# A gated cross-attention layer on one core: the step of a software pipeline rewritten on all engines, its sums done by TensorE transposes

## The reference, cut to what matters

```python
# part 1, k = v = ctx, q = layernorm(x); i, j run over the 8 rows of a head
kv  = einsum('bhil,bhjl->bijhl', k, v)
y   = causal convolution of kv with ssm_kernel[h] along l (512 taps)
out = y + kv * D
out = einsum('bijhl,bhil->bjhl', out, q)
x   = x + tanh(g_xattn) * out
# part 2, over z = layernorm(x), 16 positions per batch row, 16 heads
y = silu(z_prev * w0 + z * w1)
q = silu(y @ Wq); k = y @ Wk; v = y @ Wv; g = y @ Wg
q, k = rotary(q), rotary(k)
scores = softmax(v . router_w); onehot = one_hot(argmax(scores))   # 2 routes
norm = 1 / cumsum(onehot)
q_exp = q * scores * onehot * norm ; k_exp = k * onehot
o = tril(q_exp k_exp^T / 4) v
o = (o - mean) / sqrt(var + 1e-5)
x = x + tanh(g_ffn) * ((silu(g) * o) @ Wout)
```

## Time and profile before

| | |
|---|---|
| median of three runs | 1350.26 us (1345.44 to 1352.43) |
| span of the profiled execution (the page gives no other time of it) | 1371.8 us |
| PE busy | 1227.0 us (89%) |
| DVE busy | 1080.5 us (79%) |
| POOL busy | 849.3 us (62%) |
| ACT busy | 391.8 us (29%) |
| mean granted TensorE clock | 0.826 of 2.4 GHz |

### The profile page before, as it was taken

The page is one execution under the profiler, slowest core; times in us unless marked ns, Lnnn a source line. Parts: engine busy times, 40 slices in busy tenths (PEclk is TensorE's granted clock), DMA queues, the critical chain, the costliest instruction groups (busy, mean ns, idle before and its releaser), DMA issues.

```text
span 1371.8 us, 18443 instructions
## 1 busy us (share of the span) xinstructions
PE 1227.0 (89%) x6272; PEld 992.6 (72%) x6272; DVE 1080.5 (79%) x1815; ACT 391.8 (29%) x809; POOL 849.3 (62%) x741
## 2 busy tenths in 40 slices
PE   2579999999999999999999999999999999999986
PEld 1456878776778767778767687777788777778774
DVE  5888787778787778977779876979877779877762
ACT  3432332222332213332213322322332222332220
POOL 5667675557675557765547754767765556765520
PEclk9887798887798868988868976988888888888887
DMA  6000111110011110111110011010011010010000
GB/s 202 24 24 1 31 32 31 32 31 1 30 31 31 31 31 0 31 31 31 31 31 1 29 31 31 31 31 18 12 31 31 31 31 23 7 32 23 9 8 16
DMA packets 21579, 39.00 MB, mean 28 GB/s; under 512 B 2288, under 2 KB 3440, under 8 KB 21552
## 3 DMA queue, kind: packets, MB, share of 16 engines
q1 hardware_dynamic: 17952, 33.92, 8.7%
q10 hardware_dynamic: 3600, 4.72, 1.1%
HBM read 30.17 MB, written 8.47 MB: 28 GB/s over the span
## 4 chain that ended last, share of the span: by engine, by line
DVE 35%; PE 29%; issue 19%; POOL 12%; ACT 4%; DMA 1%; DVEq 0%; POOLq 0%; SPq 0%; ACTq 0%
PE bank L287 9%; DVE z_terms L791 8%; PE bank L339 8%; PE bank L316 6%; PE bank L276 4%; PE bank L359 3%; DVE ke L805 3%; DVE z_terms L796 2%; DVE q_sel L930 2%; POOL kv L649 2%; POOL kv_low L658 2%; DVE weight L928 2%; DVE cnt L922 2%; POOL z_terms L673 2%; DVE z_terms L785 1%
## 5 line engine op out<-in xcount | busy, mean ns | idle before, releaser
L339 PEld LDWEIGHTS bank<-v_sb,att 128*128 128x128 f32 x1024 | 246.6, 300 | 20.3
L678 POOL TENSOR_TENSOR o_rstd<-o_ve,minus_half 128x16 f32<-128x16 f32 x32 | 93.0, 2907 | 224.5 <-DVE o_ve L831 224.5
L339 PE MATMUL bank<-v_sb,att 128*128 128x32 f32 x1024 | 206.1, 342 | 0.0
L658 POOL TENSOR_TENSOR kv_low<-kv,kv_high 128x576 fp32r<-128x576 f32 x128 | 203.0, 1587 | 0.0
L678 POOL TENSOR_TENSOR rstd<-ve,minus_half 128x1 f32<-128x1 f32 x64 | 35.0, 547 | 253.8 <-DVE ve L991 221.7
L649 POOL TENSOR_TENSOR kv<-kx 128x512 f32<-128x512 f32 x128 | 177.6, 1388 | 15.1 <-ACT kx L503 15.1
L791 DVE TENSOR_TENSOR z_terms<-z_terms 128x256 f32<-128x256 f32 (+1 forms) x160 | 180.1, 1141 | 4.5 <-POOL z_terms L673 0.7
L287 PE MATMUL bank<-kv_high,toep_high 128*128 128x512 f32 x320 | 170.2, 532 | 3.4 <-DVE z_terms L785 3.4
L534 ACT ACTIVATE o_sq<-bank 128x512 f32<-128x512 f32 x32 | 19.1, 598 | 504.0 <-PE bank L339 504.0
L287 PE MATMUL bank<-kv_low,toep_high 128*128 128x512 f32 x320 | 159.9, 500 | 0.0
L287 PE MATMUL bank<-kv_high,toep_low 128*128 128x512 f32 x320 | 158.1, 494 | 0.0
(11 more groups left out here) (112 smaller groups left out, 2520.0 us busy)
## 6 DMA issues: line engine op xcount, KB each, us to landing
c_in<-in_ctx SPq DMA_DIRECT2D x32, 256.0 KB
x_in<-in_x SPq DMA_DIRECT2D x32, 256.0 KB
toep<-taps_dram SPq DMA_DIRECT2D x32, 256.0 KB, 5.2
out_x<-out_sb SPq DMA_DIRECT2D x32, 256.0 KB
w_all<-in_L_ffn_Wv ACTq DMA_DIRECT2D x1, 1024.0 KB, 11.4
w_all<-in_L_ffn_Wg ACTq DMA_DIRECT2D x1, 1024.0 KB, 8.1
w_out<-in_L_ffn_Wout ACTq DMA_DIRECT2D x1, 1024.0 KB, 12.7
router<-in_L_ffn_router_w ACTq DMA_DIRECT2D x1, 512.0 KB, 7.0
```

The costliest lines, as they stand in the source:

```text
L339: ins = nc.tensor.matmul(bank[4][:, i * HDV:(i + 1) * HDV], att[:, r, c, :], v_sb[:, i * HDV:(i + 1) * HDV], start=True, stop=True)
L658: eng.tensor_tensor(kv_p[1][:, p, c, :], kv[:, c % 2, :], kv_p[0][:, p, c, :].bitcast(F32), ALU.subtract).then_inc(kv_ready[c], 1)
L678: eng.tensor_tensor(dst[:, 0:n], src[:, 0:n], minus_half[:, 0:n], ALU.pow).then_inc(done, 1)
```

## The change

The host lays out the context (reversed, transposed, extended), so that SP loads `kx` directly, in two buffers; the ACT reversal, the PE transposes and the ACT copies go. The taps are split in high and low once, before they go to DRAM, and one DMA per step (twice the bytes) brings both; L508 and L667 go. The sums of `z_terms` on DVE and POOL go: PE transposes all eight blocks of each chunk, 32 transposes, accumulating in PSUM. The attention output is formed transposed: stationary `v_sb` 128x32, moving `att` 128x128, four column groups; ACT copies it and PE transposes it back. Scores are one block over four row groups, the attention output is one block as well, and nothing is woven. The positive factors score and 1/count leave q: the norm after the attention output cancels them if its epsilon is divided by their square, so the chain of routing instructions becomes a few with results needed later (`eps_w`), and k and q are expanded by one instruction. qn and z are formed on ACT (Identity with scale and bias) instead of DVE. x2 has four buffers. The orders of PE, ACT, POOL and DVE are new, and there is no loop: 35 steps are written out.

```diff
-            with eng.Fori(*LOOP) as t:
-                for p in range(2):
-                    step(t, p, True, True, True, True)
...
+                    if can_wait(h + 1):
+                        eng.wait_ge(conv_ps[CH - 1], h + 1)
+                        eng.wait_ge(conv_last_ps, h + 1)
+                    toeplitz(p, h + 2)
...
+            def add_transposed(h1):
+                for c in range(CH):
+                    if c == 0:
+                        eng.wait_ge(mul_last, h1 + 1)
+                    eng.wait_ge(mul_done[c], h1 + 1)
+                    for i in range(2 * NROT):
+                        ins = nc.tensor.matmul(bank[2][:, c * P:(c + 1) * P], z_terms[:, c, i * ROW:(i + 1) * ROW], ident,
+                                               is_transpose=True, start=(c == 0 and i == 0), stop=(i == 2 * NROT - 1),
+                                               skip_group_check=True)
+                ins.then_inc(xo_ps, 1)
...
+                def attention_output():
+                    for r in range(CH):
+                        eng.wait_ge(mask_done[r], h)
+                    eng.wait_ge(v_copied, h)
+                    for c in range(CH):
+                        for r in range(CH):
                             i = CH * c + r
+                            ins = nc.tensor.matmul(bank[4][r * HDV:(r + 1) * HDV, c * P:(c + 1) * P],
+                                                   v_sb[:, i * HDV:(i + 1) * HDV], att[:, r, c, :], start=True, stop=True)
+                    ins.then_inc(oT_ps, 1)
```

More of the change, by code:

```diff
@@ L112, in flamingo_gated_layer @@
         rstd2 = sb("rstd2", 1)
+        nmu2 = sb("nmu2", 1)
+        nmr2 = sb("nmr2", 1)
         z = sb("z", L)
-        d_log = sb("d_log", RH)
+        ad = sb("ad", RH)
         u = sb("u", RH)
+        sel = sb("sel", 2, RH, RATIO)
         th = sb("th", RH)
[L117 to L124, removed]
+        th1 = sb("th1", RH)
+        rth1 = sb("rth1", RH)
+        ratio = sb("ratio", RH)
+        eps_w = sb("eps_w", RH)
         o_var = sb("o_var", RH)
@@ L198, in flamingo_gated_layer @@
         mask_done = [sem(f"mask_done{i}") for i in range(CH)]
[L199 to L207, removed]
+        y_low, gatedT_ready = sem("y_low"), sem("gatedT_ready")
@@ L224, in flamingo_gated_layer @@
[L224 removed]
+        SCORE_BANKS = (2, 4, 5, 3)
         PASSES = ((0, 0), (0, 1), (1, 0))
@@ new lines, in scores @@
+                def scores():
+                    eng.wait_ge(keT_sb, h + 1)
+                    eng.wait_ge(qeT_sb, h + 1)
+                    if front:
+                        eng.wait_ge(x2_ready, h + 2)
+                    eng.wait_ge(v_copied, h + 1)
+                    for c in range(CH):
+                        for r in range(CH):
+                            rows = slice(r * 32, r * 32 + 32)
+                            ins = nc.tensor.matmul(bank[SCORE_BANKS[r]][:, c * P:(c + 1) * P], keT[rows, c, :],
+                                                   qeT[rows, c, :], start=True, stop=True)
+                            if c == CH - 1:
+                                ins.then_inc(attn_ps[r], 1)
@@ L383, in step @@
                     if can_wait(h + 1):
                         eng.wait_ge(mul_done[3], h + 1)
-                    conv(p, 1, h + 1, attention_output if woven else None, len(PASSES))
-                if tail and not woven:
-                    for n in range(PAIRS):
-                        attention_output(n)
-                if back:
-                    eng.wait_ge(z_ready, h + 1)
-                    if can_wait(h):
-                        eng.wait_ge(mask_done[1], h)
-                    transpose4(bank[7], lambda c: z[:, c * P:(c + 1) * P], zT_ps)
@@ L394, in step @@
-                if pre and back:
-                    transpose_ctx()
+                    conv(p, 1, h + 1)
+                if tail:
+                    attention_output()
                 if front:
```

578 lines of the change are left out of this document (242 added, 336 removed).

## The result

The changed kernel takes 1016.0 us (median of 4 runs, 1015.1 to 1016.5), beside 1348.0 for the kernel before in the same comparison (4 runs, 1345.4 to 1352.4): a ratio of 0.754, 95% interval 0.750 to 0.758. I had said 1110 and a range from 1030, so the direction was right and the gain was larger than anything in the range. The profiled execution spans 1014.2 us. The kernel before has fast and slow executions, 1312 to 1376 us over all the comparisons of this document, the slow ones at a lower granted clock, and its profiled execution of 1371.8 us is a slow one.

What follows compares the result with a forecast made beforehand. PE was taken as the bound, slowed by woven narrow matmuls. Work 30.1, waits 1.6 and clock 1.5 made 33.2 us a step; start 51, 31 steps and end 48 gave 1128, times 0.984 1110 us, range 1030 to 1215.

Steps and rivals of the forecast that it cites:

- changes of shape: PE, around the attention and score blocks: four changes between wide and narrow matmuls, 0.5 us a step, bounds 0 to 1.2.
- 32 accumulating transposes: PE, sums of z_terms: priced like the qn transposes at 0.105 each, 3.4 us a step; 6.2 at 1.2 GHz.
- attention block: PE, 16 attention output matmuls in the new shape: 2.0 us a step, between 1.55 and about 3.4 to 3.49.
- score block: PE, score matmuls in one block over four row groups: 1.8 us a step, 1.55 or less to 3.1.
- waits: PE waits per step: 0.4 for masks, 0.3 for o_normed, 0.9 for the gate, together 1.6 us.
- clock: PE: 36 transposes cost 3.1 us more a step if at 1.2 GHz; half of that, 1.5, was put.
- the second rival: PE clock falls twice a step, at the transposes and around the narrow blocks: 36.6 us a step, 1214 us; 16%.
- the first rival: Full clock and good overlap, attention and scores 1.5 each, waits 1.0: 30 us a step, 1030 us; 17%.
- The gate's 0.9: PE, before the k and q transposes: a wait for the gate's silu on ACT, 0.9 us a step.
- The third rival: DVE and POOL late with o_normed, so v waits 3 us: 35.5 to 36 us a step, 1190 us; 14%.
- The ends: Outside the steady steps: 51 us until the first z and 48 us after the last z starts.
- From span to time: Measured median over profiled span of the kernel before, 0.984, applied to the 1128 us span to give 1110 us.

Runs made afterwards that it cites:

- e1: The kernel before with its attention and score matmuls each in one block instead of woven, nothing else changed: 1258.7 us.
- e3: The changed kernel with attention matmuls woven into conv 2 and score matmuls into the output projection again: 1353.9 us, ratio to before 1.012.
- e10: The kernel before, still woven, with the sums of z_terms as 32 accumulating transposes on PE instead of additions on DVE and POOL: 1304.8 us.
- e5: The changed kernel with the 32 accumulating transposes done twice in a row: 1125.2 us, ratio to before 0.843.
- e6: The changed kernel with score matmuls in the earlier order, two row groups taking turns, then the other two, still one block: 1025.4 us.
- e2: The kernel before with all 35 steps written out instead of the hardware loop: 1364.0 us.
- e11: The kernel before with both blocks instead of weaving and the sums as accumulating transposes on PE: 1174.7 us.
- e4: The changed kernel with the attention output in its old shape, one block, without the oT copy and transposes back: 1100.9 us.

## Why the prediction was off

The span came out 1014.2 for 1128. The step made 31 x (33.2 - 29.35) = 119 us of that, the end 6 the other way. The step of 494 to 523 us, start to start on PE, against the terms:

| term | put | measured | |
|---|---|---|---|
| 24 single transposes | 2.5 | 2.34 | |
| conv, rank, conv_last | 8.6 | 8.84 | |
| q and k; v, g and output | 11.3 | 11.87 | |
| changes of shape | 0.5 | within the two above | |
| 32 accumulating transposes | 3.4 | 3.49 | |
| attention block | 2.0 | 1.01 | -1.0 |
| score block | 1.8 | 1.10 | -0.7 |
| waits | 1.6 | 0.78 | -0.8 |
| clock | 1.5 | 0 | -1.5 |
| step | 33.2 | 29.43 | |

- **The bound** was read rightly as PE with its woven stretches; e1 and e3 show it from both sides. Which weaving costs was not seen: at full clock the score pieces lose time and the old attention pieces lose none (e10). The 1.29 of a piece at the earlier trace rows is its own work at 1.2 GHz. That DVE was second with 33.6 us stood there too; e1 shows it was close enough to take 89 us of the gain.
- **The failed steps are the clock and the price of the two narrow blocks.** The first is the clock, 1.5 put and 0 measured. I put half of 3.1 for the chance that the transposes run at 1.2 GHz, and 16% on the second rival. e5 shows twice as many at 2.4 GHz. The Trainium skill (TensorE: Matmul & The Clock Gate, Part 4) says of transposes that the full clock does not engage for them; this case contradicts it for transposes among dense matmuls: 32 and 64 of them in a row ran at a granted 1.00, 0.109 us each. A kernel of transposes alone was not run. The four transposes of qn in the earlier trace rows had pointed that way. "The low clock goes with narrow matmuls among wide ones, not with PE idle" was read from one step. It is not a rule: e10 has the same woven attention at 1.00, and e3 has the woven attention stretch at 1.00 in 27 of 29 steps and the woven score stretch in 17.
- **The two blocks were mis-sized,** 3.8 put and 2.11 measured, and this is what left the range: its lower end came from the first rival, which has the full clock but 1.5 for each block. For both I leaned on the score block at the earlier trace rows, which overlaps two row groups. Four groups overlap better: all score matmuls of a step keep PE busy 1.17 us (37.5/32) against 1.75 (55.9/32) in e6's pairs of groups, and the 16 attention matmuls took 1.01 with small loads, under my lower end of 1.55. My upper end of 4 x 0.85 had no row of its own, as the 0.85 at the earlier trace rows is one wide matmul with two score matmuls. The estimate by the Trainium skill (same page, Part 3), 1.4 for the attention block, was nearer than my 2.0 but starts from that 3.4; the trace is lower still.
- **Changes of shape** were about right in the end: conv and projections measured 0.8 above their own rows, for 0.5. The 75.8 us behind my upper end is idle time of the weight loads (PEld), not of PE.
- **Waits.** The gate's 0.9 is there as 0.78. That for o_normed is not: v and o_normed met without a wait. Ahead of the attention block PE has a gap of some 0.25, which the table counts in the conv; whether it is the last mask's signal or the change of shape is not separated. So the walk found the right place of each and was too careful where it found no slack. The third rival, o_normed late by 3 us, did not come; POOL's power took 2.91 us as before.
- **The ends.** The start of 51 was 50.3. The end was 54.0 for 48. The last z now starts 4.7 us ahead of PE's transposes of it (960.2 to 964.9), where it was 0.6 before (1321.8 to 1322.4), and this slack counts in the end; the term had 1.5 for it. The rest of the 6 was not followed up.
- **From span to time.** I carried 0.984 over from the kernel before. That ratio only told that its profiled execution was a long one; after, it is 1016.0/1014.2 = 1.002. By luck it hid some 20 us of the miss.
- **The loads and the loop** cost nothing, as put: DMA share 0.20, and e2.
- **A slip in the second rival:** 31.7 + 3.1 + 1.5 + 1.8 is 38.1 us a step; the 1.5 that was put does not stand in the 31.7 and was taken off all the same, which gave 36.6.

What happened is the first rival in its mechanism, with the full clock and good overlap: 30 us a step by it, 29.35 measured. Steps at full clock let the gain be followed without the clock: 37.34 with the sums on PE (e10), 34.16 unwoven as well (e11), 29.43 changed. Of the last 4.7, e4 gives the attention's new shape 2.05, the wait for the routed q in e11 was 68.0/30 = 2.3, and e6 gives the scores' four groups 0.3:

```profile
PE bank L276 <- DVE qe L809: 68.0, 30, 2.8
```

These were measured apart, and that they add up is no proof of the split; the layout of the context and taps, the norms on ACT and the cancelled factors were not run alone. The step from before, 41.1 in the mean of its inner steps, to 37.34 holds together the waits for the sums and the 14.4 us a step that had run at 1.2 GHz, and what brought the clock up in it is not shown.

## What to carry to other kernels

Give narrow matmuls that use a part of the array a block of their own, in the order that lets all four groups overlap, with the small operand as the stationary one: woven between wide ones the same work cost 8 us a step more. Narrow matmuls that fill the array lost nothing by weaving at the full clock. Read the clock over all steps before you tell what lowers it: one score stretch of e3 shows 1.00 and another 0.65 for the same work. Where two engines are within 15% of each other, an edit that frees one shows a fraction of its worth alone. When the bound engine has got faster, look at once at what an in-order engine makes for it behind work that nobody is waiting for; moving that back brought 1.2 us a step here, and the 12 transposes saved 0.55 by themselves.

## What was not expected of the hardware

- Transposes that accumulate in PSUM are a cheap adder: 0.109 us for a 128x128 f32 block at 2.4 GHz, and with 64 in a row the clock is 1.00 through the steady state (e5).
- Sixteen f32 matmuls of 128 columns into four column groups took 1.01 us, 0.063 each; the same products with 128 columns loaded and 32 moved took 3.56.
- A woven pair of score matmuls, on a quarter of the array, lost 0.49 us at full clock, with no instruction in the profile to show for it. A woven pair that fills the array lost none.
- The mean clock was 0.826 with weaving and both waits (sums and routed q), 0.955 with weaving and the wait for the routed q alone (e10), 0.935 with weaving and small waits (e3), 0.888 unwoven with both waits (e1) and 0.98 with neither. So neither weaving nor waits alone go with the clock, and the old attention block brings a dip of its own in e4. What exactly lowers it stays open.
